# Transposes of the probabilities in two row halves, 12 records of 64 columns for 6 of 128

## The reference

```
# x: (32, 112, 256), context: (32, 375, 256), mask: (32, 112, 375)
q = (layer_norm(x) @ Wq)             # 16 heads of 64
k, v = split(layer_norm(context) @ Wkv)   # one head of 64, shared by all 16
sim = q @ k.T * 64 ** -0.5 + mask    # per head: 112 x 375
attn = softmax(sim, axis=-1)
out = (attn @ v) @ Wout + silu_gated_mlp(layer_norm(x))
```

## Time and profile before

| what | before |
|---|---|
| median of 3 runs | 2027.64 us (2026.38 to 2032.49) |
| the profiled execution's own time | 2031.86 us |
| its span | 2030.1 us |
| TensorE busy | 1880.4 us (93%) |
| VectorE, ScalarE, GpSimd busy | 66%, 49%, 20% |
| mean granted TensorE clock | 0.971 of full speed |

### The profile page before, as it was taken

One profiled execution on the slowest core, in us unless ns is written; L12 is line 12 of the kernel. 1 busy time (PEld: TensorE's weight loads), 2 busy tenths in 40 slices (PEclk: granted clock), 3 DMA queues, 4 the chain that ended last, 5 costly groups with the idle time before them and its releaser, 6 DMA issues.

```text
span 2030.1 us, 28540 instructions
## 1 busy us (share of the span) xinstructions
PE 1880.4 (93%) x9568; PEld 1154.3 (57%) x9568; DVE 1331.1 (66%) x4044; ACT 988.6 (49%) x2384; POOL 414.1 (20%) x569
## 2 busy tenths in 40 slices
PE   4569999999998769999999999999999999999997
PEld 2446666676676535555555555555555555555566
DVE  6667889889886256737646656755755764755744
ACT  3453553643541136644644645554554554554542
POOL 4675576576573010000000000000000000000000
PEclk8889999999999969899999999999999999999999
DMA  3000000000000172211111112111111111211100
GB/s 122 1 0 10 19 1 19 19 1 19 10 1 10 31 211 59 59 38 52 54 45 55 46 48 59 47 48 52 53 48 52 50 51 44 56 49 43 39 20 19
DMA packets 63537, 84.20 MB, mean 41 GB/s; under 512 B 5120, under 2 KB 62000, under 8 KB 62496
## 3 DMA queue, kind: packets, MB, share of 16 engines
q1 hardware_dynamic: 62928, 81.92, 14.3%
q10 hardware_dynamic: 464, 0.46, 0.1%
HBM read 75.02 MB, written 7.34 MB: 41 GB/s over the span
## 4 chain that ended last, share of the span: by engine, by line
PE 60%; DVE 3%; issue 1%; ACT 1%; DMA 0%; DVEq 0%; ACTq 0%
PE x_ps L1296 19%; PE x_ps L1251 9%; PE x_ps L1258 9%; PE x_ps L1289 8%; PE x_ps L1274 8%; PE x_ps L1365 2%; PE x_ps L1401 1%; PE x_ps L1350 1%; PE x_ps L1358 1%; PE x_ps L1371 1%; DVE x_pr L1640 1%; DVE x_bn L987 1%; PE x_ps L1437 1%; PE x_ps L1303 1%; DVE x_pr L1649 0%
## 5 line engine op out<-in xcount | busy, mean ns | idle before, releaser
L1640 DVE CUSTOM_DVE_ANT_0 x_pr<-x_ps,x_mk 128x375 f32<-128x375 f32 x448 | 228.0, 546 | 345.5 <-issue 232.9
L1511 ACT ACTIVATE x_pT<-x_ps 125x384 f32<-125x384 f32 x448 | 195.9, 489 | 349.9 <-PE x_ps L1258 348.7
L1517 ACT ACTIVATE x_pr<-x_pr,x_mx 128x375 f32<-128x375 f32 x448 | 268.1, 607 | 27.5 <-DVE x_mx L1640 27.5
L1251 PE MATMUL x_ps<-x_kT,x_qT 64*128 64x375 f32 x896 | 207.6, 538 | 22.1 <-DVE x_mx L1640 17.1
L1258 PEld LDWEIGHTS x_ps<-ident,x_pr 128*125 128x125 f32 x1344 | 166.0, 189 | 98.9 <-issue 90.8
L1258 PE MATMUL x_ps<-ident,x_pr 128*125 128x128 f32 x1344 | 208.9, 292 | 3.8 <-DVE x_pr L1649 3.8
L1296 PE MATMUL x_ps<-x_xn,x_w 128*128 128x448 f32 x512 | 203.9, 541 | 0.0
L1274 PE MATMUL x_ps<-x_pT,x_va 125*64 125x256 f32 (+1 forms) x1536 | 175.4, 364 | 0.6 <-ACT x_pT L1511 0.6
L1649 DVE TENSOR_SCALAR x_pr<-x_pr,x_rc 128x375 f32<-128x375 f32 x448 | 170.7, 424 | 8.0
L255 PE MATMUL m_ps<-m_xa,w_in 128*128 128x448 f32 x352 | 146.1, 562 | 10.2 <-ACT m_xa L454 10.2
L1251 PEld LDWEIGHTS x_ps<-x_kT,x_qT 64*128 64x128 f32 x896 | 70.1, 188 | 143.0 <-issue 114.9
(11 more groups left out here) (187 smaller groups left out, 3096.6 us busy)
## 6 DMA issues: line engine op xcount, KB each, us to landing
x_mk<-in_mask SPq DMA_DIRECT2D x224, 187.5 KB, 2.4
x_cx<-in_context SPq DMA_DIRECT2D x32, 375.0 KB
x_mixed<-m_x SPq DMA_DIRECT2D x8, 448.0 KB, 3.3
X<-x_mixed SPq DMA_DIRECT2D x8, 448.0 KB, 4.0
m_X<-in_x SPq DMA_DIRECT2D x7, 448.0 KB, 5.1
out<-f_so SPq DMA_DIRECT2D x7, 448.0 KB, 3.4
fc<-in_fc SPq DMA_DIRECT2D x2, 1024.0 KB, 11.9
x_w<-in_x_w SPq DMA_DIRECT2D x1, 2048.0 KB, 17.3
```

Of the source, the lines that this page charges most:

```text
L1251: pe.matmul(bank(e)[:, 0:J], qT[rows, b, r * ROWS:(r + 1) * ROWS], kT[rows, b % 2, :], start=True, stop=True).then_inc(h_s.sem, 1)
L1511: act.activation(pT[:, 4 * (batch(p) % 2) + 2 * (p % NP % 2) + e, :, :].rearrange("p t s -> p (t s)"), bank(2 + e)[0:JP, 0:JT * ROWS], ACT ...
L1517: act.activation(pr[:, k, :], pr[:, k, :], ACT.Exp, scale=-1.0, bias=mx[:, k:k + 1], accum_out=sums[:, k:k + 1]).then_inc(h_e.sem, 1)
L1640: dve.tensor_tensor_reduce(pr[:, k + e, :], bank(e)[:, 0:J], mk[:, p % SLOT, :], -1.0, 3.0e38, ALU.add, ALU.min, mx[:, k + e:k + e + 1]).t ...
```

## The change

The same transposes are issued by row half `g` of the probabilities. For each unit `k` and piece `t` there are now two transposes: rows 0 to 63 and rows 64 to 127, each with a stationary operand of 64 rows by 125 columns and 64 moving columns of the identity. Half g of both units goes to bank 2+g: 6 blocks of 64 columns. The copies on ScalarE go by row half too: each reads 384 columns of a bank and writes six runs of 64 elements, for both units at once. `turn` waits once for both units to be divided and once for both copies of the step before; `highest` waits for both halves of the step that used its buffer.

```diff
@@ -1251,12 +1251,16 @@
             def turn(i, p):
-                for e in range(2):
-                    pe.wait_ge(h_n.sem, h_n.value(i, 2 * p + e + 1))
-                    hold(pe, h_c, i, 2 * p + e - 1)
+
+                pe.wait_ge(h_n.sem, h_n.value(i, 2 * p + 2))
+                hold(pe, h_c, i, 2 * p)
+                for k in range(2):
                     for t in range(JT):
-                        last = pe.transpose(bank(2 + e)[0:JP, t * ROWS:(t + 1) * ROWS], pr[:, 2 * (p % SLOT) + e, t * JP:(t + 1) * JP], ident[:, :])
-                    last.then_inc(h_t.sem, 1)
+                        for g in range(2):
+                            rows, at = slice(64 * g, 64 * g + 64), (k * JT + t) * 64
+                            last = pe.transpose(bank(2 + g)[0:JP, at:at + 64], pr[rows, 2 * (p % SLOT) + k, t * JP:(t + 1) * JP], ident[rows, rows])
+                            if k == 1 and t == JT - 1:
+                                last.then_inc(h_t.sem, 1)
@@ -1503,12 +1507,13 @@
             def copies(i, p):
-                for e in range(2):
-                    u = 2 * p + e
-                    act.wait_ge(h_t.sem, h_t.value(i, u + 1))
-                    if e == 0 and p % NP % 2 == 0:
+                k = 4 * (batch(p) % 2) + 2 * (p % NP % 2)
+                for g in range(2):
+                    act.wait_ge(h_t.sem, h_t.value(i, 2 * p + g + 1))
+                    if g == 0 and p % NP % 2 == 0:
                         hold(act, h_o, i, batch(p) - 1)
-                    act.activation(pT[:, 4 * (batch(p) % 2) + 2 * (p % NP % 2) + e, :, :].rearrange("p t s -> p (t s)"), bank(2 + e)[0:JP, 0:JT * ROWS], ACT.Copy).then_inc(h_c.sem, 1)
+                    act.activation(pT[:, k:k + 2, :, 64 * g:64 * g + 64].rearrange("p e t s -> p (e t) s"),
+                                   bank(2 + g)[0:JP, 0:2 * JT * 64].rearrange("p (x s) -> p x s", s=64), ACT.Copy).then_inc(h_c.sem, 1)
@@ -1636,7 +1641,8 @@
                     dve.wait_ge(h_s.sem, h_s.value(i, u + 1))
-                    hold(dve, h_t, i, u + 1 - 2 * SLOT)
+                    if e == 0:
+                        hold(dve, h_t, i, 2 * (p - SLOT) + 2)
```

## The result

The changed kernel takes 2036.84 us (median of 11 runs, 2031.85 to 2042.86) against 2029.20 for the kernel before in the same rounds: ratio 1.0032, 95% interval 1.0018 to 1.0047, that is 4 to 10 us slower, 6.5 us at its middle (the two medians lie 7.6 apart). The forecast was +4.0 and, on the median of the first three runs, 2031.6 us. All ratios in this document leave out one execution in a slow state, of 4827.62 us, which was one of the four of experiment 2.

The account below looks back on a forecast made before the run. TensorE's own stream was taken to bound the kernel. Edges at switches of operand kind summed to +3.7 us, the last copies added +0.3: +4.0, or 2031.6 us on the median, range 2026 to 2041 us.

Parts of the forecast that it names:

- TensorE's stream sets the time, and the inside of a run of transposes does not change: In `turn`: five intervals stay at 0.109 us, 0.545 in all, because loading 125 columns sets the pace.
- The halves run side by side if issued in pairs: In `turn`: both row halves load and move side by side, the second some 7 ns behind the first.
- the rival without pairing: In `turn`: twelve single transposes run one behind the other at 0.109, +0.65 us a call, 2175 us; chance 0.04.
- Behind `times_v` -0.049: First pair of `turn` after `times_v` ends 0.25 us behind it instead of 0.30; -0.049 us with the 7 ns.
- behind `scores` -0.243: First pair of `turn` after `scores` ends 0.054 us behind it instead of 0.30; -0.243 us with the 7 ns.
- ahead of `vback` -0.138: From `turn` to `vback`: 0.11 us instead of 0.25, -0.138 us.
- Ahead of a piece of kind F +0.195: From `turn` to a piece with over 64 rows and columns of stationary operand: a new surcharge of 0.195 us.
- The copies, hidden but for the end, +0.3: ScalarE's first copy starts about 0.3 us later, hidden except after the last `turn`, where it costs +0.3 us.
- The first group and the clock: First group: later `turn` starts priced at 0, up to +2 us for the range; clock left to a rival.
- the rival of the clock: First group: 10 us more at the lower clock cost about 4 us, 2035.6; chance 0.17 together with slower pace.

Follow-up runs that it names:

- experiment 2: Changed kernel with transposes loading windows of 128 columns of stationary operand instead of 125: 1986.16 us, ratio 0.9783 to the kernel before.
- 6: Changed kernel with transposes loading windows of 126 columns of stationary operand instead of 125: 1989.24 us, one run.
- 7: Changed kernel with transposes loading windows of 127 columns of stationary operand instead of 125: 2035.89 us, one run.
- experiment 1: Kernel before, whole transposes, with 128 columns of stationary operand instead of 125: 2019.70 us, ratio 0.9956.
- experiment 3: Changed kernel with the six transposes of rows 0 to 63 issued before the six of rows 64 to 127: 2087.07 us, ratio 1.0290.
- the two traces: Changed kernel, unedited, profiled twice: 2036.84 us, ratio 1.0032, and once more 2037.54 us, ratio 1.0037.
- with filler: Extra useless TensorE matmuls in the first group, in both kernels: kernel before 2030.23 us, ratio 0.9998; changed kernel 2032.30 us, ratio 1.0012.

## Why the prediction was right, and where not

- **TensorE's stream sets the time, and the inside of a run of transposes does not change.** Right, and shown three ways: the interval is 0.109 in both kernels, it falls to 0.062 when the load gets faster (experiments 2 and 6), and it comes back, to 0.111, with one more column (7). The reason given, that the moving columns "were not what took the time", is half of it: by experiment 1 whole transposes stay at 0.11 with the fast load too. Either bound alone holds that pace, so halving one of them buys nothing, and halving both does.
- **The halves run side by side if issued in pairs.** Right; experiment 3 goes part of the way to the rival without pairing, 1.03 us for twelve where that rival has some 1.4.
- **Behind `times_v` -0.049, behind `scores` -0.243, ahead of `vback` -0.138.** Right: -0.052, -0.251 and -0.139 by the medians of the two traces.
- **Ahead of a piece of kind F +0.195.** This is the term that was mis-sized. It holds ahead of full fp32 matmuls, where it was read. Ahead of context and token transposes, 69 of the 176 cases, it is 0.148. The likely reason comes out of experiments 1, 6 and 7: the surcharge has the next load in it, and those transposes have an even count of columns. Their load records are 141 ns, those of a full fp32 matmul 190: 0.049 less, where the surcharge is 0.047 less. The rest of it is some 0.09 us by an estimate: 0.195 less the 0.109 at which loads of 125 columns follow each other, or 0.148 less the 0.062 of 128 columns. The mistake was to take a surcharge read ahead of one kind of record for all. With 0.148 the sum of the edges falls by 69 x 0.047 = 3.2 us, from +3.7 to +0.5. The same correction takes a middle group from +0.5 to 0.10, where 0.12 was measured; that it comes so near is partly luck, since step 19's wait (+0.14) and slightly larger savings at the other edges (-0.13 together) cancel.
- **The copies, hidden but for the end, +0.3.** The end is right, +0.27. "Bare once" is wrong: the late copies also hold up `x_cT` and with it `kv` in step 19 of each middle group, +0.14 each, some 1 us in all. The prediction asked only when `times_v` needs the copies, not what ScalarE does behind them.
- **The first group and the clock.** The forecast put nothing there and gave the clock a part of a rival. By the start of `scores` in the two first traces, the change's lag grew by 0.8 us ahead of the attention (code that the change doesn't touch), by 2.9 with the stretch at the lower clock, by 0.7 in groups 2 to 7, 0.3 in group 8 and 0.5 behind it; that and the rest of the first group make the 5.5 of the spans. So the rival of the clock came true beside the forecast's mechanism.

Of the measured 6.5 us, then, some 2 are the change's edges and its late copies: 0.4 in the first group (with filler), 0.7 in groups 2 to 7, 0.9 from there to the end. The rest is time at the lower clock, most of it in the first group. All executions with a clock on record point the same way: the changed kernel's 18 have a mean granted clock of 0.9686 of full speed, the 71 of the kernel before 0.9715. A fit of time to clock and kernel through these 89 gives 1.5 us for each 0.001 of mean clock and, at equal clock, 2.1 us (1.0 to 3.3) for the change. The forecast of +4.0 was near because an overpriced edge, an unseen wait and an unpriced clock offset each other; that is luck. What stays open is why the clock falls near 778 us in some executions of the changed kernel and not in others.

Of the rules weighed: by the Trainium skill's "TensorE: Matmul & The Clock Gate", section "LDWEIGHTS (loading the stationary operand)", the time of a load goes with its column count. The records of 125 columns in transposes (188 ns) and of 128 in full fp32 matmuls (190 ns) agree. The transposes of an even count don't: 128 columns have records of 139 ns and lie 0.062 us apart where 125 lie 0.109, and there the measurement decides. The rule of the Trainium skill's "TensorEngine Tiling (Array Packing)", section "Key Properties", that a change of tiling mode drains the engine, fits the surcharge at each switch seen here (0.14 to 0.195 us); no run shows the drain itself.

## What to carry to other kernels

Before splitting small matmuls or transposes, find which of the two sets their distance, the moving operand or the load of the stationary one: compare two runs in the same trace that share one and differ in the other. If both give the same distance, as here, both have to shrink. Count the switches between row-split, column-split and whole operands along TensorE's stream, price each from a row with the same kind behind it, and put pieces of one kind side by side; here that order turned a loss of 0.3% into a gain of 0.6%. When an engine off the critical path starts later, look at everything that it does behind the late piece. In fp32 transposes like these, try an even number of columns of stationary operand, if need be by reading a few of the neighbour's.

## What was not expected of the hardware

- The load for an fp32 transpose is shorter with 112, 126 or 128 columns than with 125 or 127: the mean record is 134 to 142 ns against 188, and pairs in row halves lie 0.062 us apart against 0.109. For 125 and 128 columns that is so with 64 and with 128 rows alike. It moves the whole kernel by 47 us in row halves (1989 against 2036 us, one run each).
- The halves overlap only in part if issued one behind the other: in pairs twelve transposes take 0.77 us, half behind half 1.03.
- With shorter `turn`s where TensorE already waits, its granted clock was lower for the next 3 to 7 us in two traces (0.69 and 0.84 in a window that stood at 1.00 before). That the shorter work caused it is likely, not shown.
